# Expert rows turned by VectorE in 32x32 blocks, and first-layer expert weights read as one 8 KB run per partition

## The chip, the cores and the metric

The kernel runs on one core of a Trainium2 chip. The metric is the device time of one execution in microseconds (us), lower is better. Three runs of the kernel before took 1007.83, 1006.43 and 1007.63 us; the median is 1007.63 us.

## The reference, cut to what matters

Two decoder layers over x of shape (8, 100, 512), all float32: self-attention, cross-attention to a context of 722 rows, and a feed-forward part, each followed by a residual and a layer norm. The change lies in the feed-forward part of the first layer, a mixture of 8 experts. Each of the 800 rows picks its two best experts by a softmax gate. An expert is three 512x512 layers:

    h1 = relu(row @ w1[e] + b1[e])
    h2 = relu(h1 @ w2[e] + b2[e])
    y  = relu(gate * (h2 @ w3[e] + b3[e]))

The kernel needs the sum of y over the rows of a tile of one expert, and hands that sum back to every row that chose the expert.

## The kernel before, in words

The whole program is one sequence of blocks. A block gives each engine its own instruction list; the engines meet at a barrier at its end. This case concerns two neighbouring blocks.

**The routing block** (from line 1784). The gate is computed, the 800 rows (512 features and 8 gate values, so XW = 520 floats or 2080 bytes) are scattered into DRAM by expert (`rows_dram`), and a table gives for each of MT = 20 tiles of 128 rows its expert and its first row. Under this, TensorE folds weights of a later layer (`fold_one`, lines 1899 to 1941). SyncE (the SP queue) loads the weights of the first three units, waits for the scatter and for the fold step "bvo", and then issues `gather(0)` to `gather(5)` (AHEAD = 6, lines 1995 to 2003). `gather` (line 1780) reads the tile's row number from the table and copies 128 whole rows into SBUF, one row to a partition, by one DMA.

**The expert block** (from line 2044). Each tile i goes through three layers l. The 60 pairs (i, l) are the units. They are ordered on a slant (line 1676): after the start, units repeat as (i,0), (i-1,1), (i-2,2), which is called a round here. For i of 1 and more, unit (i,0) is number 3(i-1). The weights of a unit are 1 MB, w[e] of 512x512, in a ring of six slots; SP loads unit n when unit n-6 is made (`load_unit`, lines 1684 and 2055). `expert_w` (line 1675) splits the 512 input features as chunk c, partition p, feature 128c+p, so a partition gets four runs of 2 KB. After the load, from n = 5 on, SP issues one more gather per unit until all 20 are out, then one of six loads for the next stage per unit (`last`, lines 2047 to 2063).

For a matrix product over features, the features must lie on the partitions, but a gathered tile has rows there. So TensorE turns tile i by four 128x128 transposes into PSUM (`turn`, line 2069), ScalarE copies them to `xh` (`keep`, line 2143), and the first layer waits for the semaphore `kept`. The order on TensorE is written out by hand: ahead of the unit before (i,0), it does `turn(i)` (lines 2118 to 2121). A unit is `layer(n)` (line 2102): 4 output chunks times 4 feature chunks, 16 matmuls of 128x128 by 128. ScalarE applies bias and relu after layer 0 (line 2155), VectorE after layer 1 (`second_layer`, line 2198), and VectorE adds bias and multiplies by the gate after layer 2 (`weigh`, line 2213). GpSimd picks the gate values of a tile (line 2247), VectorE sums them (`gate_of`), and TensorE spreads them by one small matmul at each l = 1 unit (`spread_gate`, line 2084). From unit 39 on (PREP_AT), ScalarE and VectorE also prepare weights of the next stage: `in_kv` is waited for by VectorE at n = 39 and `in_qup` by ScalarE at n = 40.

Of the kernel before, what the change touches and what calls it, by code (L numbers as in the profile page):

```python
# [23 lines left out]
P = 128  # L24
# [90 lines left out]
def program(nc, g, out):  # L115
    ctx = ExitStack()
    with ctx:
# [1557 lines left out]
        expert_w = [g[f"L0_ffn_w{i}"].rearrange("e (c p) o -> p e c o", p=P) for i in (1, 2, 3)]  # L1675
# [89 lines left out]
        AHEAD = 6  # L1765
# [12 lines left out]
        gathered = [sem(f"rows_gathered{i}") for i in range(MT)]  # L1778

        def gather(sp, i):  # L1780
            row = sp.value_load(table[0:1, 1, i:i + 1], min_val=0, max_val=SPARE)
            sp.dma_start(rows_of_tile(i), rows_dram[bass.ds(row, P), :]).then_inc(gathered[i], 16)

        with nc.Block() as block:
# [210 lines left out]
            @block.sync  # L1995
            def _(sp):
                sp.wait_ge(chain, CH["table"])
                for n in range(NL):
                    load_unit(sp, n, expert_of(sp, units[n][0]))
                sp.wait_ge(scattered, 16 * 2 * B)  # L2000
                sp.wait_ge(folded, fold_at["bvo", 0] + 1)
                for i in range(AHEAD):
                    gather(sp, i)
# [13 lines left out]
        xh, h1, h2 = (sb("ffn_" + n, [P, 2, C, P], F32, ff) for n in ("xh", "h1", "h2"))  # L2017
# [5 lines left out]
        turned, kept, made, h1_kept, h2_kept, gated, gate_col, gate_rows, rows_kept, weighed, counted, v_flip, v_hi, v_lo, by_tile, tile_kept = (  # L2023
            sem("ffn_" + s) for s in ("turned", "kept", "made", "h1_kept", "h2_kept", "gated", "gate_col", "gate_rows",
# [10 lines left out]
        def unit_made(eng, i, l):  # L2035

            eng.wait_ge(made, unit_at[i, l] + 1)
# [6 lines left out]
        with nc.Block() as block:  # L2044
            @block.sync
            def _(sp):
                last = [(rk, natural(g["L1_attn_Wk"]), in_kv), (rv, natural(g["L1_attn_Wv"]), in_kv),
                        (rd, g["L1_attn_W_down_kv"].rearrange("(c p) l -> p c l", p=P), in_qup),
                        (ru, g["L1_attn_W_up_k"].rearrange("l (c d) -> l c d", c=C), in_qup),
                        (rw, g["L1_attn_W_up_v"].rearrange("l (c d) -> l c d", c=C), in_qup),  # L2050
                        (rq, natural(g["L1_attn_Wq"]), in_qup)]
                more = AHEAD
                for n in range(NL, len(units)):
                    expert = expert_of(sp, units[n][0])
                    if n >= SLOTS:
                        sp.wait_ge(made, n - SLOTS + 1)
                    load_unit(sp, n, expert)
                    if n >= SLOTS - 1 and more < MT:
                        gather(sp, more)
                        more += 1  # L2060
                    elif more == MT and last:
                        to, src, landed = last.pop(0)
                        sp.dma_start(to if to is rw else to[:], src).then_inc(landed, 16)
                for s in range(SLOTS):
                    sp.wait_ge(w_landed[s], 16 * (len(units) // SLOTS))

            @block.tensor
            def _(pe):
                def turn(i):
                    pe.wait_ge(gathered[i], 16)  # L2070
                    if i >= 2:
                        pe.wait_ge(kept, i - 1)
                    for c in range(C):
                        mm = nc.tensor.transpose(ps[:, 3 + i % 2, c * P:(c + 1) * P], rows_of_tile(i)[:, c * P:(c + 1) * P],  # L2074
                                                 ident[:, :])
                    mm.then_inc(turned, 1)

# [24 lines left out]
                def layer(n):  # L2102
# [6 lines left out]
                    for m in range(C):  # L2109
                        for k in range(C):  # L2110
                            if l and m == 0:
                                pe.wait_ge((h1_kept, h2_kept)[l - 1], C * i + k + 1)
                            mm = nc.tensor.matmul(acc(n)[:, m, :], w[:, n % SLOTS, k, m * P:(m + 1) * P],  # L2113
                                                  into[l][:, i % 2, k, :], start=k == 0, stop=k == C - 1,
# [3 lines left out]
                turn(0)  # L2118
                for n, (i, l) in enumerate(units):
                    if n + 1 < len(units) and units[n + 1][1] == 0:  # L2120
                        turn(units[n + 1][0])
# [20 lines left out]
            def _(act):  # L2142
                def keep(i):
                    act.wait_ge(turned, i + 1)
                    if i >= 2:
                        unit_made(act, i - 2, 0)
                    nc.scalar.activation(xh[:, i % 2, :, :], ps[:, 3 + i % 2, :].rearrange("p (c t) -> p c t", c=C),  # L2147
                                         ACT.Identity).then_inc(kept, 1)

# [14 lines left out]
                keep(0)  # L2164
                for n, (i, l) in enumerate(units):
                    if n + 1 < len(units) and units[n + 1][1] == 0:
                        keep(units[n + 1][0])
# [29 lines left out]
            def _(dve):  # L2197
                def second_layer(n, i):
# [22 lines left out]

                for n, (i, l) in enumerate(units):
                    if l == 0:
# [18 lines left out]
            def _(pool):  # L2242
                for i in range(MT):
                    pool.wait_ge(gathered[i], 16)
# [871 lines left out]
```

## Time and profile before, and how to read it

| what | value |
| --- | --- |
| median of three runs | 1007.63 us |
| span of the profiled execution, first to last instruction | 1003.7 us |
| TensorE busy over the span (matmuls, weight loads) | 934.0 us (93%), 757.2 us (75%) |
| VectorE, ScalarE, GpSimd busy | 429.3, 346.5, 250.9 us |
| mean granted TensorE clock over the span | 0.957 of full |
| data moved by DMA | 162.01 MB, mean 161 GB/s |

The profiled execution has no time of its own beside its span of 1003.7 us; the median of the runs lies 3.9 us above that span, which is time around the first and last instruction. PE is TensorE's matmul side, PEld its weight loads, DVE VectorE, ACT ScalarE, POOL GpSimd, SPq the queue of SyncE. A float32 matmul shows as two PE and two PEld records (passes), so a unit has 32 of each. Matmuls are pipelined and their ends are modelled: the distance between starts says what one costs, not its duration.

### The profile page before, as it was taken

How to read it: one execution, taken by the hardware profiler on the slowest of the kernel's cores; microseconds unless marked ns; L12 is line 12 of the kernel's file. 1: busy time of each engine (PE TensorE's matmuls, PEld its weight loads, DVE VectorE, ACT ScalarE, POOL GpSimd, SP SyncE). 2: the span in 40 equal slices, each digit the busy share in tenths (PEclk: the TensorE clock that was granted, in tenths of full speed). 3: DMA queues.
4: the chain of work that ended last, by engine and by line, in shares of the span. 5: the costliest groups of instructions: out<-in, count | busy, mean ns of one | idle time of the engine just before them, and what ended most of it. 6: DMA issues, size and time to landing. Idle time of an engine off the chain costs nothing. (4 is left out here: it accounts for less than half of the span.)

```text
span 1003.7 us, 19227 instructions
## 1 busy us (share of the span) xinstructions
PE 934.0 (93%) x7747; PEld 757.2 (75%) x7747; DVE 429.3 (43%) x994; ACT 346.5 (35%) x886; POOL 250.9 (25%) x306
## 2 busy tenths in 40 slices
PE   5999999989998889999999999999889899999994
PEld 5977776676775644789999999987765578999532
DVE  2973454224442647002112132135267630656576
ACT  2322323245552124122222233324276611122374
POOL 5452111023554306000000010004065403000275
PEclk9999999999999979899999999997969998999996
DMA  9994000245622807259999888700040032971001
GB/s 254 382 331 127 2 2 2 98 152 203 238 120 95 309 7 254 55 181 386 358 383 313 284 269 283 254 29 28 4 153 3 2 119 78 321 247 66 1 15 51
DMA packets 72456, 162.01 MB, mean 161 GB/s; under 512 B 4132, under 2 KB 5685, under 8 KB 70321
## 3 DMA queue, kind: packets, MB, share of 16 engines
q1 hardware_dynamic: 70048, 156.54, 45.8%
q0 software_dynamic: 2320, 4.25, 1.4%
q8 instruction: 61, 1.00, 0.4%
q14 instruction: 27, 0.21, 0.1%
HBM read 128.81 MB, written 31.97 MB: 160 GB/s over the span
## 5 line engine op out<-in xcount | busy, mean ns | idle before, releaser
L2113 PE MATMUL ps<-ffn_h,ffn_w 128*128 128x128 f32 x1280 | 149.1, 275 | 0.0
L2113 PEld LDWEIGHTS ps<-ffn_h,ffn_w 128*128 128x128 f32 x1280 | 145.9, 192 | 0.0
L2113 PE MATMUL ps<-ffn_xh,ffn_w 128*128 128x128 f32 x640 | 74.9, 275 | 0.3 <-ACT ffn_xh L2147 0.3
L2203 DVE TENSOR_SCALAR ffn_h<-ps,tile_bias 128x128 f32<-128x128 f32 x80 | 22.5, 345 | 122.4 <-PE ps L2113 122.4
L2113 PEld LDWEIGHTS ps<-ffn_xh,ffn_w 128*128 128x128 f32 x640 | 73.1, 192 | 0.9 <-issue 0.9
L1418 POOL TENSOR_TENSOR ctx_low<-shelf,ctx_high 128x1024 fp32r<-128x1024 f32 (+2 forms) x24 | 43.0, 1819 | 65.4 <-PE ps L1283 33.7
L2161 ACT ACTIVATE ffn_y<-ffn_y 128x128 f32<-128x128 f32 x80 | 23.7, 298 | 73.9 <-DVE ffn_y L2219 73.9
L1526 PE MATMUL ps<-x_qT,ctx_ct 128*128 128x100 f32 (+1 forms) x384 | 46.4, 284 | 2.3 <-PEq L137 2.0
L1526 PEld LDWEIGHTS ps<-x_qT,ctx_ct 128*128 128x128 f32 (+1 forms) x384 | 45.0, 197 | 3.7 <-issue 3.2
L2219 DVE SCALAR_TENSOR_TENSOR ffn_y<-ps,tile_bias,ffn_gate_row 128x128 f32<-128x128 f32 x80 | 22.6, 344 | 58.0 <-PE ps L2113 57.9
L2834 POOL TENSOR_TENSOR att_e<-att_e,decay 100x400 f32<-100x400 f32 x32 | 32.7, 1033 | 46.1 <-DVE att_e L2685 46.1
L111 PE MATMUL ps<-ctx_ct,x_qT 128*100 128x210 f32 (+1 forms) x128 | 40.3, 467 | 1.0 <-DVE ctx_ct L1432 0.7
L2155 ACT ACTIVATE ffn_h<-ps,tile_bias 128x128 f32<-128x128 f32 x80 | 22.8, 368 | 41.6 <-PE ps L2113 41.6
L3007 POOL TENSOR_TENSOR rstd<-rstd,minus_half 100x1 f32<-100x1 f32 x16 | 11.6, 740 | 99.6 <-DVE rstd L2950 95.0
L111 PEld LDWEIGHTS ps<-ctx_ct,x_qT 128*100 128x100 f32 x128 | 20.6, 166 | 18.7 <-issue 17.4
L2781 ACT ACTIVATE att_e<-att_e,att_mx 100x100 f32<-100x100 f32 x96 | 28.1, 365 | 15.5 <-DVE att_mx L2690 15.5
L1538 PE MATMUL ps<-ctx_pT,shelf 128*128 128x100 f32 (+1 forms) x288 | 33.2, 275 | 0.2 <-ACT xf L1571 0.2
L1538 PEld LDWEIGHTS ps<-ctx_pT,shelf 128*128 128x128 f32 (+1 forms) x288 | 32.6, 192 | 0.4 <-issue 0.4
L1565 ACT ACTIVATE ctx_pk<-ctx_pk,ctx_st 128x100 f32<-128x100 f32 x48 | 13.8, 365 | 54.9 <-DVE ctx_st L1601 54.9
L2906 PE MATMUL ps<-x_n,xf 128*100 128x512 f32 x64 | 29.9, 596 | 0.6 <-PEq L1507 0.6
L111 PE MATMUL ps<-l_ro,xf 128*100 128x512 f32 x64 | 29.7, 608 | 0.0
L2147 ACT ACTIVATE ffn_xh<-ps 128x512 f32<-128x512 f32 x20 | 11.8, 598 | 49.1 <-PE ps L2074 49.1
(469 smaller groups left out, 2096.8 us busy)
## 6 DMA issues: line engine op xcount, KB each, us to landing
ffn_w<-in_L_ffn_w_dram SPq DMA_DIRECT2D x60, 1024.0 KB, 6.0
shelf<-in_ctx_dram SPq DMA_DIRECT2D x12, 1280.0 KB
expert_rows<-nothing SPq DMA_DIRECT2D x1, 14820.0 KB, 49.6
context_turned<-ctx_ct SPq DMA_DIRECT2D x8, 1444.0 KB, 7.9
ctx_ct<-context_turned SPq DMA_DIRECT2D x8, 1444.0 KB, 12.5
ctx_lent<-in_ctx_dram SPq DMA_DIRECT2D x4, 1280.0 KB
rows_own<-expert_rows SPq DMA_DIRECT2D x8, 260.0 KB, 3.0
x_wo<-in_L_xattn_Wo_dram SPq DMA_DIRECT2D x1, 2048.0 KB, 9.5
```

The costliest lines, as they stand in the source:

```text
L111: last = pe.matmul(out, a, b, start=(n == 0), stop=(n == len(products) - 1))
L1418: nc.gpsimd.tensor_tensor(raw_low[b % RAWS][0:rows_, j0:j1, :], raw[b % RAWS][0:rows_, j0:j1, :], raw_high[b % 2][0:rows_, j0:j1, :].bitca ...
L1526: mm = nc.tensor.matmul(ps[0:rows_, SB + i, (j - j0) * T:(j - j0 + 1) * T], ct[b % 2][:, k, j * P:j * P + rows_], qT[:, k, b * T:(b + 1) * T],
L1538: mm = nc.tensor.matmul(ps[:, VB, c * T:(c + 1) * T], raw[b % RAWS][0:keys(j), j, c * P:(c + 1) * P], pT[0:keys(j), b % 2, j, :], start=j ...
L2113: mm = nc.tensor.matmul(acc(n)[:, m, :], w[:, n % SLOTS, k, m * P:(m + 1) * P], into[l][:, i % 2, k, :], start=k == 0, stop=k == C - 1, sk ...
L2155: nc.scalar.activation(h1[:, i % 2, m, :], acc(n)[:, m, :], ACT.Relu, bias=bsel[:, m, i, 0:1]).then_inc(h1_kept, 1)
L2161: nc.scalar.activation(y[:, i % 2, m, :], y[:, i % 2, m, :], ACT.Relu, accum_out=vT[:, m, i:i + 1]).then_inc(counted, 1)
L2203: nc.vector.tensor_scalar(h2[:, i % 2, m, :], acc(n)[:, m, :], bsel[:, m, i, 1:2], 0.0, ALU.add, ALU.max).then_inc(h2_kept, 1)
L2219: nc.vector.scalar_tensor_tensor(y[:, i % 2, m, :], acc(n)[:, m, :], bsel[:, m, i, 2:3], gate_row[:, i % 2, :], ALU.add, ALU.mult).then_in ...
L2781: ins = nc.scalar.activation(e[:, c, :], e[:, c, :], ACT.Exp, bias=mx[:, b % 2, r, c:c + 1])
L2834: nc.gpsimd.tensor_tensor(e, e, decay[:, :].unsqueeze(1).to_broadcast([T, C, T]), ALU.mult).then_inc(faded, 1)
L2906: mm = nc.tensor.matmul(ps[0:T, b % 3, :], xf[:, k, b * T:(b + 1) * T], n1[:, k, :], start=k == 0, stop=False)
```

## The change: what it does

- The DMA of a tile's features is cut into four, one per group f of 32 partitions. Each writes 32 partitions with four pieces of 512 bytes: partition 32f+r gets, for i = 0 to 3, features 128f to 128f+127 of row 32i+r. A fifth DMA brings the 8 gate values of each row (32 bytes a partition), with a semaphore of its own that GpSimd waits for.
- VectorE then turns the 16 blocks of 32x32 in one instruction. It reads the features with a step of four (16 bytes), so that after it partition p holds, for chunk k, feature 4p+k of all 128 rows. `xh` is laid out as [partition, row group, chunk, 32].
- The first layer's weights are split the same way, feature 4p+k, so that partition p gets rows 4p to 4p+3 of w1 as one run of 8 KB. Its matmuls read `xh` as four runs of 32 floats. The other two layers are unchanged.
- TensorE's `turn` and ScalarE's `keep` are gone, and the PSUM banks 3 and 4 with them.
- Three tiles are gathered in the routing block in place of six. The rest follow one per round, at the l = 1 units from n = 4 on; the six `last` loads follow at the l = 2 units 26, 29, ... 41.

```diff
-        expert_w = [g[f"L0_ffn_w{i}"].rearrange("e (c p) o -> p e c o", p=P) for i in (1, 2, 3)]
+        first_w = g["L0_ffn_w1"].rearrange("e (p c) o -> p e c o", c=C)
+        group = lambda f: slice(f * HD, (f + 1) * HD)
+        expert_w = [first_w] + [g[f"L0_ffn_w{i}"].rearrange("e (c p) o -> p e c o", p=P) for i in (2, 3)]
...
-        AHEAD = 6
+        AHEAD, EARLY = 6, 3
...
         def gather(sp, i):
             row = sp.value_load(table[0:1, 1, i:i + 1], min_val=0, max_val=SPARE)
-            sp.dma_start(rows_of_tile(i), rows_dram[bass.ds(row, P), :]).then_inc(gathered[i], 16)
+            here = rows_dram[bass.ds(row, P), :]
+            for f in range(HPC):
+                sp.dma_start(rows_of_tile(i)[group(f), 0:D].rearrange("r (i d) -> r i d", d=P),
+                             here[:, f * P:(f + 1) * P].rearrange("(i r) d -> r i d", r=HD)).then_inc(gathered[i], 16)
+            sp.dma_start(rows_of_tile(i)[:, D:XW], here[:, D:XW]).then_inc(gathered_gates[i], 16)
...
-                for i in range(AHEAD):
+                for i in range(EARLY):
                     gather(sp, i)
...
-        xh, h1, h2 = (sb("ffn_" + n, [P, 2, C, P], F32, ff) for n in ("xh", "h1", "h2"))
+        xh = sb("ffn_xh", [P, 2, HPC, C, HD], F32, ff)
+        h1, h2 = (sb("ffn_" + n, [P, 2, C, P], F32, ff) for n in ("h1", "h2"))
...
-                    if n >= SLOTS - 1 and more < MT:
+                    if more < MT and units[n][1] == 1:
                         gather(sp, more)
                         more += 1
-                    elif more == MT and last:
+                    elif n >= 4 * SLOTS and units[n][1] == 2 and last:
                         to, src, landed = last.pop(0)
...
-                def turn(i):
-                    pe.wait_ge(gathered[i], 16)
-                    if i >= 2:
-                        pe.wait_ge(kept, i - 1)
-                    for c in range(C):
-                        mm = nc.tensor.transpose(ps[:, 3 + i % 2, c * P:(c + 1) * P], rows_of_tile(i)[:, c * P:(c + 1) * P],
-                                                 ident[:, :])
-                    mm.then_inc(turned, 1)
...
+                            rhs = xh[:, i % 2, :, k, :] if l == 0 else into[l][:, i % 2, k, :]
                             mm = nc.tensor.matmul(acc(n)[:, m, :], w[:, n % SLOTS, k, m * P:(m + 1) * P],
-                                                  into[l][:, i % 2, k, :], start=k == 0, stop=k == C - 1,
+                                                  rhs, start=k == 0, stop=k == C - 1,
...
-                def keep(i):
-                    act.wait_ge(turned, i + 1)
-                    if i >= 2:
-                        unit_made(act, i - 2, 0)
-                    nc.scalar.activation(xh[:, i % 2, :, :], ps[:, 3 + i % 2, :].rearrange("p (c t) -> p c t", c=C),
-                                         ACT.Identity).then_inc(kept, 1)
...
+                def turn(i):
+                    dve.wait_ge(gathered[i], 16 * HPC)
+                    if i >= 2:
+                        unit_made(dve, i - 2, 0)
+                    nc.vector.transpose(xh[:, i % 2], rows_of_tile(i)[:, 0:D].rearrange("p (i d k) -> p i k d", i=HPC, k=C)
+                                        ).then_inc(kept, 1)
...
+                turn(0)
                 for n, (i, l) in enumerate(units):
+                    if n + 1 < len(units) and units[n + 1][1] == 0:
+                        turn(units[n + 1][0])
                     if l == 0:
                         gate_of(i)
...
-                    pool.wait_ge(gathered[i], 16)
+                    pool.wait_ge(gathered_gates[i], 16)
```

## Rows read from the trace of the kernel before

**Rows 1.** Busy time by stage: stretch, length, then each engine, clock, DMA share, GB/s.

```profile
core 0: us, PE busy (x) PEld busy (x) DVE busy (x) ACT busy (x) POOL busy (x), PEclk, DMA share, GB/s
439.00:672.00 233.00, 232.62 (x2080) 231.94 (x2081) 52.03 (x183) 68.71 (x290) 5.45 (x16) 1.00 0.85 291
```

**Rows 2.** Timeline of one round: start, duration, engine, line, operation, count, idle before.

```profile
481.56 0.60 PE L2074 MATMUL ps<-ident,rows_own 128*128 128x128 f32 x4
481.76 1.13 DVE L2203 TENSOR_SCALAR ffn_h<-ps,tile_bias 128x128 f32<-128x128 f32 x4 [6.11 <-PE ps L2113]
...
482.00 3.74 PE L2113 MATMUL ps<-ffn_h,ffn_w 128*128 128x128 f32 x32
...
485.57 3.74 PE L2113 MATMUL ps<-ffn_xh,ffn_w 128*128 128x128 f32 x32
...
489.14 0.39 PE L2084 MATMUL ps<-ident,ffn_gate 128*128 128x128 f32 x2
...
489.37 3.74 PE L2113 MATMUL ps<-ffn_h,ffn_w 128*128 128x128 f32 x32
```

**Rows 3.** Timeline of PE where the expert block begins.

```profile
436.57 0.40 PE L111 MATMUL ps<-x_wk_hi,x_wq_lo 128*128 128x512 f32 x1
437.90 1.07 PE L2074 MATMUL ps<-ident,rows_own 128*128 128x128 f32 x8 [0.94 <-PEq L1784]
439.31 0.91 PE L2113 MATMUL ps<-ffn_xh,ffn_w 128*128 128x128 f32 x6 [0.34 <-ACT ffn_xh L2147]
```

**Rows 4.** Instructions on the copied tile: duration min/median/max in ns, first and last start.

```profile
L2147 ACT ACTIVATE ffn_xh<-ps x20: 592/597/614, 438.6 to 642.8; 128x512 f32<-128x512 f32 x20
```

**Rows 5.** Timeline of DVE in the expert block, other work of its kind.

```profile
589.40 2.28 DVE L2231 TENSOR_TENSOR l_raw_k<-l_raw_k,l_raw_v 128x2048 f32<-128x2048 f32 x1
...
600.71 0.68 DVE L2236 TENSOR_TENSOR l_pu_lo<-l_raw_up_k,l_pu_hi 128x512 fp32r<-128x512 f32 x1
...
607.98 1.22 DVE L2236 TENSOR_TENSOR l_pq_lo<-l_raw_q,l_pq_hi 128x1024 fp32r<-128x1024 f32 x1
```

**Rows 6.** Timeline of PEld in the routing block, weight loads between float32 passes of 512 columns.

```profile
400.43 0.19 PEld L111 LDWEIGHTS ps<-x_woT,x_wv 128*128 128x128 f32 x1 [0.24 <-issue]
...
400.86 0.19 PEld L111 LDWEIGHTS ps<-x_woT,x_wv 128*128 128x128 f32 x1 [0.24 <-issue]
```

**Rows 7.** DMA issues of SP in time order: table reads between them, and none.

```profile
419.48 5.86 SPq L1782 DMA_DIRECT2D rows_own<-expert_rows  x6
438.57 2.69 SPq L1687 DMA_DIRECT2D ffn_w<-in_L_ffn_w_dram  x3
...
674.06 0.42 SPq L2256 DMA_DIRECT2D spreads<-in_spreads_dram  x1
674.53 0.43 SPq L2257 DMA_DIRECT2D l_ro<-in_L_attn_Wo_dram  x1
```

**Rows 8.** Issue to landing, page: weights, row tiles, the last load (KB each, median us).

```profile
ffn_w<-in_L_ffn_w_dram SPq DMA_DIRECT2D x60, 1024.0 KB, 6.0
...
xT_hi<-expert_rows SPq DMA_DIRECT2D x6, 260.0 KB, 8.3
...
l_raw_q<-in_L_attn_Wq_dram SPq DMA_DIRECT2D x1, 1024.0 KB, 12.3
```

**Rows 9.** DMA from 450 to 470 us: 2 KB runs, engines full.

```profile
q1 hardware_dynamic: 3947, 7.72, 104.6%
```

**Rows 10.** DMA from 674.5 to 675.1 us: 128 runs of 512 bytes and 16 smaller.

```profile
q1 hardware_dynamic: 144, 0.07, 37.6%
```

**Rows 11.** DMA from 815 to 832 us: runs of 11.5 KB.

```profile
q1 hardware_dynamic: 288, 2.96, 47.9%
```

**Rows 12.** Busy time and clock after a pause of PE, columns as in rows 1.

```profile
677.00:678.00 1.00, 0.00 (x0) 0.00 (x0) 0.93 (x3) 0.58 (x1) 0.28 (x2) 1.00 1.02 375
678.00:680.00 2.00, 1.71 (x6) 1.02 (x6) 1.61 (x4) 0.73 (x2) 1.26 (x4) 0.50 0.64 240
...
684.00:690.00 6.00, 5.13 (x17) 3.51 (x17) 4.82 (x10) 3.51 (x6) 2.51 (x9) 0.50 0.00 0
```

More of the change, by code:

```diff
@@ L1777, in program @@
         fold_bank = lambda n: ps[:, (7, 0, 1)[n % 3], :]
-        gathered = [sem(f"rows_gathered{i}") for i in range(MT)]
+        gathered, gathered_gates = ([sem(f"{what}_gathered{i}") for i in range(MT)] for what in ("rows", "gates"))
         def gather(sp, i):
             row = sp.value_load(table[0:1, 1, i:i + 1], min_val=0, max_val=SPARE)
-            sp.dma_start(rows_of_tile(i), rows_dram[bass.ds(row, P), :]).then_inc(gathered[i], 16)
+            here = rows_dram[bass.ds(row, P), :]
[3 more added lines that the diff above has]
+            sp.dma_start(rows_of_tile(i)[:, D:XW], here[:, D:XW]).then_inc(gathered_gates[i], 16)
         with nc.Block() as block:
@@ L2022, in program @@
         vT = sb("ffn_vT", [P, C, MT], F32, ff)
-        turned, kept, made, h1_kept, h2_kept, gated, gate_col, gate_rows, rows_kept, weighed, counted, v_flip, v_hi, v_lo, by_tile, tile_kept = (
-            sem("ffn_" + s) for s in ("turned", "kept", "made", "h1_kept", "h2_kept", "gated", "gate_col", "gate_rows",
+        kept, made, h1_kept, h2_kept, gated, gate_col, gate_rows, rows_kept, weighed, counted, v_flip, v_hi, v_lo, by_tile, tile_kept = (
+            sem("ffn_" + s) for s in ("kept", "made", "h1_kept", "h2_kept", "gated", "gate_col", "gate_rows",
                                       "rows_kept", "weighed", "counted", "v_flip", "v_hi", "v_lo", "by_tile", "tile_kept"))
@@ L2051, in _ @@
                         (rq, natural(g["L1_attn_Wq"]), in_qup)]
-                more = AHEAD
+                more = EARLY
                 for n in range(NL, len(units)):
@@ L2057, in _ @@
                     load_unit(sp, n, expert)
-                    if n >= SLOTS - 1 and more < MT:
+                    if more < MT and units[n][1] == 1:
                         gather(sp, more)
                         more += 1
-                    elif more == MT and last:
+                    elif n >= 4 * SLOTS and units[n][1] == 2 and last:
                         to, src, landed = last.pop(0)
                         sp.dma_start(to if to is rw else to[:], src).then_inc(landed, 16)
+                assert more == MT and not last
                 for s in range(SLOTS):
@@ L2112, in layer @@
                                 pe.wait_ge((h1_kept, h2_kept)[l - 1], C * i + k + 1)
+                            rhs = xh[:, i % 2, :, k, :] if l == 0 else into[l][:, i % 2, k, :]
                             mm = nc.tensor.matmul(acc(n)[:, m, :], w[:, n % SLOTS, k, m * P:(m + 1) * P],
-                                                  into[l][:, i % 2, k, :], start=k == 0, stop=k == C - 1,
+                                                  rhs, start=k == 0, stop=k == C - 1,
                                                   skip_group_check=True)
                     mm.then_inc(made, 1)
-                turn(0)
                 for n, (i, l) in enumerate(units):
-                    if n + 1 < len(units) and units[n + 1][1] == 0:
-                        turn(units[n + 1][0])
                     if l == 1:
@@ L2162, in total @@
                                              accum_out=vT[:, m, i:i + 1]).then_inc(counted, 1)
-                keep(0)
                 for n, (i, l) in enumerate(units):
-                    if n + 1 < len(units) and units[n + 1][1] == 0:
-                        keep(units[n + 1][0])
                     if 0 <= n - PREP_AT - 1 < len(PREP):
```

## The prediction

> **What bounds the kernel now.** I read the busy time by stage first. From 439 to 672 us the expert block runs, and there TensorE's matmuls are busy 232.62 of 233 us at full granted clock (1.00) while VectorE is busy 52 us and ScalarE 69 us; the 16 DMA engines show a share of 0.85 [rows 1]. So this block lasts as long as TensorE's own list of instructions, and something taken off that list shortens it if nothing else comes to the front. Then I read the timeline of one round for what each entry of that list costs [rows 2]. The reader should look at starts: a unit takes 485.57 - 482.00 = 3.57 us, and so does the next (489.14 - 485.57). The four transposes of a turn hold the list from 481.56 to 482.00, 0.44 us. The gate's small matmul holds it from 489.14 to 489.37, 0.23 us. A round is 3 x 3.57 + 0.44 + 0.23 = 11.38 us. Third, the beginning of the block: the last pass of the routing block starts at 436.57 and ends at 436.97, TensorE goes on at 437.90 with two turns, and the first unit starts at 439.31, after ScalarE's copy [rows 3]. That copy starts at 438.6 and takes 0.60 us [rows 4], so from its end to the first pass there is about 0.1 us.
>
> **Part 1, the turns leave TensorE.** Of 20 turns, 18 lie between units; each gives back 0.44 us: 18 x 0.44 = 7.9 us. This is on the path that sets the end, since TensorE has no idle time there to absorb it. A round becomes 10.94 us.
>
> **Part 2, the start.** Turns 0 and 1 lie ahead of the first unit. In the changed kernel the first unit waits for VectorE's first turn, which can begin when the barrier opens, as TensorE does now at 437.90. The trace has no turn on VectorE. Its nearest rows: one instruction over 512 elements a partition from SBUF takes 0.68 us, over 1024 elements 1.22, over 2048 elements 2.28 [rows 5]. I take 0.69 us, by the row with the same 512 elements. The bounds: from half of that, were two elements moved at a time, to 2.28, were each element of the stepped read to cost as much as four. With 0.69 and the hop of 0.1, the first unit starts at 438.69 in place of 439.31: 0.6 us gained, with bounds from 0.95 gained to 0.97 lost.
>
> **Part 3, where the later turns lie on VectorE.** Turn i stands behind the four instructions of `second_layer` and ahead of `weigh`. In rows 2 `second_layer` starts 0.20 us after the unit before it is done (481.76 against 481.56) and lasts 1.13. The next first layer is due 3.57 us after the same point. That leaves 3.57 - 1.33 - 0.10 = 2.14 us for a turn, so 0.69 us is hidden by the unit of layer 2 that TensorE runs meanwhile; without that cover each turn would cost its full length. One place is tighter: the preparation of later weights puts 1.22 us between, starting at 607.98 [rows 5], which is 0.20 + 1.04 = 1.24 us after a unit is done (the four instructions of `second_layer` take 1.13 us with the end of the last). The turn is done at 607.98 + 1.22 + 0.69 + 0.10 = 609.99, while the unit is due near 607.98 - 1.24 + 3.57 = 610.31. It still fits. VectorE waits now for the gather; behind that wait stand `weigh` and `gate_of`, and for these ScalarE's sums and the gate matmul, so a late tile would hold the whole chain. ScalarE loses 20 copies of 0.60 us, which nobody on the path waited for: nothing.
>
> **Part 4, the gathers on SP.** With a table read between, DMA issues stand (5.86 - 0.35) / 5 = 1.1 us apart, loads (2.69 - 0.38) / 2 = 1.16; without one, 674.53 - 674.06 = 0.47 [rows 7]. A gather of five DMAs is 1.1 + 4 x 0.47 = 3.0 us, at most 5.5 if each costs 1.1. In the routing block, three take 9 us (at most 16.5) from 419.48, so they are out before TensorE's last pass ends at 436.97 [rows 3, 7]: nothing, the fold matmuls are the cover. In the expert block a round asks SP for 3 loads and one gather, 3.5 + 3.0 = 6.5 us (at most 9.0) of 10.94: the queue keeps up, and a load behind a gather goes out up to 0.6 us late. Tile i is issued when unit 3i-11 is made and turned after unit 3i-5: six units, 21 us, against 3 to 5.5 us of issue and 8.3 us of landing [rows 8]. Hidden.
>
> **Part 5, what the DMA engines carry.** A weight load has five units, 17.9 us, from issue to use and lands in 6.0 [rows 8], so 11.9 us are to spare. That is why the 8 KB run itself is worth nothing here. Per packet: full engines spent 1.046 x 16 x 20 us / 3947 = 85 ns on a 2 KB run [rows 9]; a 512-byte run alone cost 0.376 x 16 x 0.6 / 144 = 25 ns [rows 10]; a run of 10.3 KB on average 0.479 x 16 x 17 / 288 = 452 ns [rows 11], so 8 KB some 360. A round then asks (1024 x 85 + 128 x 360 + 640 x 25) / 16 = 9.3 us of each engine, in 10.94: nothing. The six loads for the next stage add at most 512 x 85 / 16 = 2.7 us to a round, which the 11.9 us absorb. The last of them goes out when unit 35 is made and is needed after unit 39: 14.3 us against the 12.3 that it took to land among other traffic [rows 8]. It fits.
>
> **Part 6, the passes over four runs of 32.** No row shows a matmul that reads its moving operand in runs. Four passes of 128 columns take 4 x 3.57 / 32 = 0.446 us, one of 512 columns 400.86 - 400.43 = 0.43 [rows 2, 6], so a break between instructions costs 5 ns at most. If a break between runs cost as much, three in each of 640 first-layer passes are 640 x 3 x 5 = 10 us; a gain is excluded, since no column falls away. I take nothing: a new instruction brings new weights, a new run only a new address.
>
> **The sum**, against the profiled execution: 7.9 + 0.6 = 8.5 us from its span of 1003.7 gives 995.2. The runs' median lies 3.9 us above that span, and I keep this: **999.1 us**.
>
> **The rivals.** *The clock falls at the start.* TensorE now pauses from 436.97 to 438.69, 1.7 us, in place of 0.9 and 0.3. After 677 us a pause of about that length is followed by a clock of 0.50 up to 690 [rows 12], that is 1.2 in place of 2.4 GHz. Were it so here for up to 12 us, up to 6 us would be lost; I price it at 4, the forecast becoming 1003. Against it: the same place had 0.9 and 0.3 us of pause before, and the block ran at 1.00 all the same [rows 1, 3]. *The turn is slow.* VectorE reads with a step of 16 bytes. At 2.28 us the start loses 0.97, each of the 18 later turns is 0.14 late, 2.5 in all, and the tight place 1.3: 7.9 - 0.97 - 2.5 - 1.3 = 3.1 us gained, about 1004.5. At 1.22 us only about 0.7 of the 8.5 us would go. No row shows a stepped read of this kind. The Trainium skill, Advanced Engine Details and Errata, section SBUF Cachelines, says that SBUF answers in lines of 16 bytes and that a read whose every access falls in a new line pays for it, which speaks against this change. It states no price; rows 5 show dense reads only. *The small packets starve the weights*, the case on the slower side. Its place is the DMA engines between 447 and 640 us. If a packet of a gather costs p ns among other traffic, a round asks 8.3 + 0.040 p us, and 17 rounds with a gather run 17 x (8.3 + 0.040 p - 10.94) us into arrears, of which 11.9 are covered. It eats the gain of 8.5 from p = 96 ns on, and at 110 ns the kernel takes 1017 us. For it: VectorE, SP and TensorE would all wait behind one late tile. Against it: 25 ns alone [rows 10], and even the 85 ns of a 2 KB run on full engines [rows 9] leave the gain nearly whole. *The runs cost a break each* (part 6): at the whole 10 us the result is 1009.
>
> **How the numbers follow.** The forecast has 0.71, the clock 0.10, the slow turn 0.08, the small packets 0.06, the runs 0.05. A measurement of this kernel can tell about 0.2%, 2 us, from no change. The first three cases are all faster by more: 0.89, of which I move 0.01 to the others for what I have not seen; the runs' case splits between same and slower. So faster 0.88, same 0.03, slower 0.09. The range reaches from 996.5, the forecast with the better start and the spread of 1.4 us of the runs, to 1004.5, which holds the clock and the slow turn and leaves the last two out.
>
> **What would show it.** No transposes on TensorE between 439 and 664 us, and passes of a unit still 3.57 us apart, in first layers too. A round of 10.94. One instruction of VectorE per tile, near 0.69 us, ended before the unit that needs it is due. The first unit near 438.7, at clock 1.00. Weight loads landing well within 17.9 us. I am wrong if TensorE shows idle time ahead of first layers (named after VectorE or a gather), if it waits for weights, or if first-layer passes are wider apart than the others.

## The result, and the profile after

The changed kernel takes **999.76 us** in the median of 11 runs (995.55 to 1004.6); the kernel before, run beside it, 1006.86 us. The ratio is 0.9942, 95% interval [0.9922, 0.9963]; it is formed from the runs, while the quotient of the two medians is 0.9930. The forecast was 999.1 us. In two later sets of runs on one chip each, the same kernel stood at 0.9929 [0.9909, 0.9948] and 0.9912 [0.9887, 0.9937] to the kernel before. (Of the 11 runs of before, one took 2871.49 us and was disturbed; without it their median is 1006.65 us.)

The profiled execution took 995.55 us with a span of 993.8. First, TensorE's list of one round, and VectorE's turn beside it, from the timeline of the changed kernel (start, duration, engine, line, operation, count, idle time before):

```profile
493.42 1.09 DVE L2191 STREAM_TRANSPOSE ffn_xh<-rows_own 128x512 f32<-128x512 f32 x1
...
495.75 3.74 PE L2114 MATMUL ps<-ffn_xh,ffn_w 128*128 128x128 f32 x32
...
499.32 0.39 PE L2084 MATMUL ps<-ident,ffn_gate 128*128 128x128 f32 x2
...
503.32 1.13 DVE L2199 TENSOR_SCALAR ffn_h<-ps,tile_bias 128x128 f32<-128x128 f32 x4 [6.08 <-PE ps L2114]
504.36 1.09 DVE L2191 STREAM_TRANSPOSE ffn_xh<-rows_own 128x512 f32<-128x512 f32 x1
```

The transposes of [rows 2] are gone from PE. A first-layer unit still holds the list for 499.32 - 495.75 = 3.57 us, so its four runs of 32 columns cost nothing. With the gate's 0.22 and two more units the next first layer is due 10.94 us later, at 506.69; the turn for it ends at 504.36 + 1.09 = 505.45. It is hidden, with 1.2 us to spare.

Second, the same timeline where the expert block begins, where it ends, and at VectorE's first turns:

```profile
436.11 0.40 PE L111 MATMUL ps<-x_wk_hi,x_wq_lo 128*128 128x512 f32 x1
438.67 5.44 PE L2114 MATMUL ps<-ffn_xh,ffn_w 128*128 128x128 f32 x32 [2.16 <-DVE ffn_xh L2191]
444.04 0.54 PE L2129 MATMUL ps<-indT,tile_expert_turned 8*20 8x400 f32 x2
...
664.68 0.61 PE L2135 MATMUL ps<-ident,ffn_vT 128*20 128x128 f32 x4
```

```profile
437.45 2.05 DVE L2191 STREAM_TRANSPOSE ffn_xh<-rows_own 128x512 f32<-128x512 f32 x2 [42.92 <-PEq L1791]
```

This answers to [rows 3]. TensorE stands still for 2.16 us in place of 0.94 and 0.34, and then the first unit holds the list for 444.04 - 438.67 = 5.37 us; in a kernel without that pause it takes 3.74 (below). The busy time by stage says why (stretch, length, busy time of PE, PEld, DVE, ACT, POOL, granted clock, DMA share, GB/s):

```profile
438.00:439.00 1.00, 0.33 (x2) 0.36 (x2) 1.00 (x2) 0.00 (x0) 0.00 (x0) 0.85 0.00 0
439.00:442.00 3.00, 3.00 (x16) 3.00 (x16) 0.61 (x3) 0.00 (x0) 0.20 (x1) 0.50 0.97 322
442.00:444.00 2.00, 2.00 (x18) 1.91 (x17) 0.00 (x0) 0.00 (x0) 0.00 (x0) 0.97 0.75 274
444.00:600.00 156.00, 156.00 (x1395) 155.61 (x1395) 49.10 (x139) 41.04 (x189) 3.19 (x14) 1.00 1.04 336
```

The granted clock is 0.50 (1.2 of 2.4 GHz) from about the start of the first unit and back at 1.00 shortly after 442 us, before that unit ends. From there TensorE is busy without a gap up to 600 us. The DMA share is 1.04, where before it was 0.97 from 446 to 600 us. The page's row on the weight loads, from issue to landing (KB each, median us), stands against 6.0 in [rows 8]:

```profile
ffn_w<-in_L_ffn_w_dram SPq DMA_DIRECT2D x60, 1024.0 KB, 9.6
```

The slowest took 14.1 us, of the 17.9 that a load has.

**Where the 9.9 us between the two profiled spans went.** I use three landmarks: the end of the routing block's last pass, the first unit, and the last transposes of the block, on `ffn_vT`. The row for these in the timeline of PE of the kernel before:

```profile
671.43 0.60 PE L2137 MATMUL ps<-ident,ffn_vT 128*20 128x128 f32 x4
```

| stretch | before | after | gained |
| --- | --- | --- | --- |
| span's start to the last pass's end | 436.97 | 436.51 | 0.46 |
| that pass to the first unit | 2.34 | 2.16 | 0.18 |
| first unit to the last transposes | 232.12 | 226.01 | 6.11 |
| last transposes to the span's end | 332.27 | 329.12 | 3.15 |

Only the second and third rows, 6.29 us, belong to the change. The first is where the routing block happened to end (435.0 to 440.8 us in the 13 profiles of this study). The 0.46 us were there before the change can act: the gate's matmuls, at the head of the block, start at 352.83 us before and at 352.30 after, and from there to the last pass's end it is 84.14 and 84.21 us. Part of that spread is the clock too. In the changed kernel's first profile it fell to 0.50 while a pause of 2.38 us near 363 us still ran; in its second it fell only some 2.6 us after the end of the same pause, and there the same way took 87.01 us. The last row is, in these two profiles, a fall of the clock at another barrier, 170 us behind the change, which some executions have and some don't, whatever the kernel. Timeline of PE there, before and then after, and busy time over ten microseconds of it, columns as above, again before and then after:

```profile
841.83 8.62 PE L1526 MATMUL ps<-x_qT,ctx_ct 128*128 128x100 f32 x48 [1.97 <-PEq L137]
```

```profile
834.82 5.37 PE L1526 MATMUL ps<-x_qT,ctx_ct 128*128 128x100 f32 x48 [1.97 <-PEq L137]
```

```profile
840.00:850.00 10.00, 8.17 (x45) 8.20 (x46) 0.39 (x3) 0.49 (x1) 8.19 (x7) 0.66 0.41 147
```

```profile
830.00:840.00 10.00, 8.03 (x64) 7.73 (x62) 0.65 (x3) 1.19 (x2) 5.20 (x5) 1.00 0.39 128
```

The same 48 matmuls after the same pause of 1.97 us took 8.62 us or 5.37: 3.25 us. In the 13 profiles they took 8.6 us six times, 7.0 twice and 5.4 five times, at a mean clock of 0.60, 0.76 and 1.00. In all 13 profiles the last stretch is 332.2 to 332.3 us (five times, two of them the changed kernel's repeats), 331.1 to 331.4 (three) or 328.6 to 329.1 (five); one of the middle three had the 8.6 us and was quicker elsewhere. So a comparison of two profiled spans is worth 3 us more or less by this alone, and below, the stretch from the first unit to the last transposes, called the **stage** here, is what is compared. It holds what the first unit loses.

6.29 us of 1006.86 would be a ratio of 0.9938. The first two intervals hold it, the third ends at 0.9937.

### The profile page after: what moved, and what is told of

Its sections match the earlier page's. It is cut to its first block and busy times, and to the rows that moved or that the text cites. A ratio compares the mean times of both kernels' runs of the same rounds, so it can differ in the third digit from the quotient of the medians.

```text
span 993.8 us, 19289 instructions
## 1 busy us (share of the span) xinstructions
PE 923.1 (93%) x7667; PEld 746.0 (75%) x7667; DVE 450.0 (45%) x1014; ACT 335.4 (34%) x866; POOL 249.5 (25%) x306
## 5 line engine op out<-in xcount | busy, mean ns | idle before, releaser
L2114 PE MATMUL ps<-ffn_h,ffn_w 128*128 128x128 f32 x1280 | 146.4, 275 | 0.0
L1526 PE MATMUL ps<-x_qT,ctx_ct 128*128 128x100 f32 (+1 forms) x384 | 43.1, 272 | 2.3 <-PEq L137 2.0
L1526 PEld LDWEIGHTS ps<-x_qT,ctx_ct 128*128 128x128 f32 (+1 forms) x384 | 41.7, 185 | 3.7 <-issue 3.2
L2191 DVE STREAM_TRANSPOSE ffn_xh<-rows_own 128x512 f32<-128x512 f32 x8 | 8.6, 1087 | 47.5 <-PEq L1791 42.9
```

What stands on the lines that cost most here:

```text
L1526: mm = nc.tensor.matmul(ps[0:rows_, SB + i, (j - j0) * T:(j - j0 + 1) * T], ct[b % 2][:, k, j * P:j * P + rows_], qT[:, k, b * T:(b + 1) * T],
```

## The experiments

The theory after this reading: the turns are gone as forecast and hidden on VectorE; what is missing is the pause at the start, through the clock (theory A). The rival was that the DMA engines, now full, delay loads or tiles (theory B). The change again (its first run), the first early turn, the busy TensorE and the whole rows ran on one chip, beside the kernel before at 1005.33 us; the dense and the doubled turn, the four runs and the 8 KB run alone beside it at 1005.41; the other three kernels on another chip, beside it at 1006.37.

**The change again.** The changed kernel unedited, twice, to stand beside the others.

> The changed kernel once more, unaltered, for a second profile. Theory A (the pause): after the barrier TensorE stands idle for about 2.2 us until VectorE has turned tile 0, its clock then drops to half, and the first unit takes about 5.4 us in place of 3.57; the rest of the block runs at 10.94 us a round, and the stage from the first unit to the last transposes of the block is about 226 us again. Theory B (the small packets): the DMA engines are full, and in some executions weights or tiles come late; then this profile shows TensorE waiting for weights or for VectorE inside the block, in another place than the start. The time against before lies between 0.992 and 0.996 by either.

> The changed kernel once more, to stand beside the run above: pause 2.16 us, first unit 5.4 us long, 226.0 us from first unit to last transposes, about 999 us, ratio to before near 0.9935.

Measured: 998.74 us, ratio 0.9929 [0.9909, 0.9948], pause 2.16 us, stage 666.05 - 440.03 = 226.02; then 999.4 us, 0.9912 [0.9887, 0.9937], pause 2.17, stage 669.00 - 442.99 = 226.01. The stage repeats to 0.01 us, the total does not (the runs spread over 993.98 to 1003.01). A loss that is the same to 0.01 us each time is not one of chance traffic on the DMA engines.

**The first two turns earlier.** VectorE turns tiles 0 and 1 at the end of its list in the routing block, when they have landed, and the expert block begins with the matmuls. (`xh` and the semaphore `kept` are made earlier for this, which the cut leaves out.)

```diff
+                for i in range(2):
+                    dve.wait_ge(gathered[i], 16 * HPC)
+                    nc.vector.transpose(xh[:, i], rows_of_tile(i)[:, 0:D].rearrange("p (i d k) -> p i k d", i=HPC, k=C)
+                                        ).then_inc(kept, 1)
...
-                turn(0)
                 for n, (i, l) in enumerate(units):
-                    if n + 1 < len(units) and units[n + 1][1] == 0:
+                    if 1 < n + 1 < len(units) and units[n + 1][1] == 0 and units[n + 1][0] >= 2:
```

> Tiles 0 and 1 are turned at the end of the routing block's VectorE list, under the fold matmuls, so the first unit waits for the barrier alone. Theory A: TensorE's pause falls from 2.2 to about 1 us, the first unit starts some 1.1 us earlier after the barrier's opening, the clock stays at 1.00 and the first unit takes 3.57 us: 1.1 + 1.8 = 2.9 us less than the changed kernel. Theory B: only the 1.1 us of the start, or nothing, since the time that is missing is lost at the DMA engines.

> The kernel with the first two turns made in the routing block, a second time. Theory A (the pause of 2.16 us costs 1.63 us of clock, and the turn itself another 1.07 of the gap): first unit about 1.1 us after the last pass of the routing block, at clock 1.00, 224.4 us from the first unit to the last transposes; 2.7 us less than the changed kernel beside it, ratio to before near 0.991, but the 5 us by which runs of one kernel differ can hide part of this. Rival (what was gained the first time was chance): the two medians within 1 us.

Measured: 995.25 us, ratio 0.9917 [0.9887, 0.9947]; the second time 994.89, 0.9887 [0.9871, 0.9903], beside 999.4 for the changed kernel. Timeline of PE, and busy time over the first unit, of the first of them:

```profile
439.08 3.81 PE L2118 MATMUL ps<-ffn_xh,ffn_w 128*128 128x128 f32 x32 [1.09 <-PEq L1792]
442.82 0.53 PE L2133 MATMUL ps<-indT,tile_expert_turned 8*20 8x400 f32 x2
...
663.46 0.61 PE L2139 MATMUL ps<-ident,ffn_vT 128*20 128x128 f32 x4
```

```profile
439.08:442.82 3.74, 3.74 (x32) 3.62 (x32) 0.32 (x2) 0.00 (x0) 0.41 (x3) 1.00 0.55 166
```

The pause is the barrier's 1.09 us alone, the clock stays at 1.00, the first unit takes 3.74 us, and the stage is 663.46 - 439.08 = 224.38 us: 1.63 less than 226.01, as theory A says, with as many gathers and as full engines (a share of 1.05 from 446 to 600 us, against 1.04). With the pause, 1.63 + 1.07 = 2.7 us. The medians differ by 3.5 and 4.5 us; the part above 2.7 lies within what runs of one kernel differ by. This version is the fastest of the study.

The second profile of it shows theory B too, once. Its stage is 225.14 us; timeline of PE:

```profile
593.27 3.84 PE L2118 MATMUL ps<-ffn_xh,ffn_w 128*128 128x128 f32 x32 [0.29 <-DMA ffn_w<-in_L_ffn_w_dram]
...
597.17 7.64 PE L2118 MATMUL ps<-ffn_h,ffn_w 128*128 128x128 f32 x64
604.64 3.74 PE L2118 MATMUL ps<-ffn_xh,ffn_w 128*128 128x128 f32 x32
```

A weight load came 0.3 us late, and two units behind it took 604.64 - 597.17 = 7.47 us in place of 7.14, with PEld waiting for a load as well. The longest landing there was 15.4 us. Part of it is SP's queue: the load for the unit at 593.27 could go out when the unit that starts at 570.92 is made, at 574.5, but SP was at a gather from 571.18 to 576.17 and at two more loads, and issued it at 580.00, 5.5 us late. So the loads are in time with little in hand near 590 us, where the loads for the next stage ride along; it cost some 0.76 us in this one execution, and nothing in the other profiles of kernels with this kind of gather and one turn a tile.

**TensorE kept busy through the wait.** The turns stay where the change put them; ten small matmuls (128x128 by 128) whose result nobody uses stand ahead of the units on TensorE.

```diff
+                keep_array_busy(10)
                 for n, (i, l) in enumerate(units):
                     if l == 1:
                         spread_gate(i)
```

> TensorE multiplies ten 128x128 blocks that nobody reads before it waits for the first turn; everything else is the changed kernel. Theory A: the first unit starts when it did (about 1.2 us after VectorE's turn begins), but the clock stays at 1.00 and the unit takes 3.57 us: 1.8 us less than the changed kernel. If the pause has nothing to do with the clock, the first unit still takes about 5.4 us and the time is the changed kernel's.

Measured: 997.26 us, ratio 0.9925 [0.9901, 0.9949], against 998.74 for the changed kernel on the same chip. Timeline of PE:

```profile
434.58 0.40 PE L111 MATMUL ps<-x_wk_hi,x_wq_lo 128*128 128x512 f32 x1
435.91 1.30 PE L553 MATMUL ps<-identR 128*128 128x128 f32 x10 [0.94 <-PEq L1791]
437.15 3.81 PE L2114 MATMUL ps<-ffn_xh,ffn_w 128*128 128x128 f32 x32
...
661.54 0.61 PE L2136 MATMUL ps<-ident,ffn_vT 128*20 128x128 f32 x4
```

The first unit comes 437.15 - 434.98 = 2.17 us after the last pass, as late as in the changed kernel, and yet the clock stays at 1.00 and the stage is 661.54 - 437.15 = 224.39. So the 1.63 us are the clock's alone, not those of tiles or weights that arrive late. This is what the kernel before had without meaning to: its turns stood in the same place [rows 3]. The matmuls leave TensorE idle for only 2.17 - 1.24 = 0.93 us there, so the runs do not tell whether the longest pause or the sum of the pauses counts.

**A pause between.** The early turn, with a VectorE copy that TensorE waits for before its first unit.

```diff
+                pe.wait_ge(paused, 1)
                 for n, (i, l) in enumerate(units):
...
+                nc.vector.tensor_copy(spare[:, :, :, :], xh[:, 0, 0:2]).then_inc(paused, 1)
```

> The early turn, with TensorE made to wait once more at the start for a VectorE copy of 256 elements a partition (an added instruction, whose result nobody uses) so that the pause is about 1.5 us, between the 1.09 after which the clock stayed at 1.00 and the 1.80 after which it fell. Theory A (what decides is how long TensorE stands still): either the first unit takes 3.7 us and the stage 224.4, or 5.4 and 226.0; the run says which side 1.5 us lies on. Rival (the fall comes from waiting for the turn or from what VectorE does, not from the length of the pause): the stage stays at 224.4 whatever the pause.

Measured, in one execution: the pause came out at 1.33 us, not 1.5, the clock stayed at 1.00 and the stage is 666.07 - 441.66 = 224.41. So waiting for VectorE does not by itself cost the clock; but as 1.33 us cost nothing, this run alone does not part theory A from the rival. The busy TensorE does: VectorE did the same turns there, and the clock stayed. In this place 1.33 us cost nothing and 1.80 (next experiment) cost the full 1.63. Between them it is open, and it holds for this place alone: at the later barrier 1.97 us went both ways, and behind the expert block eleven of the 13 profiles have a pause of 1.6 us and a clock of 0.50 after it ([rows 12] is one), while in the other two the clock was down already ahead of it.

**The same turn, read densely.** Each block reads 32 features side by side. One execution.

```diff
-                    nc.vector.transpose(xh[:, i % 2], rows_of_tile(i)[:, 0:D].rearrange("p (i d k) -> p i k d", i=HPC, k=C)
+                    nc.vector.transpose(xh[:, i % 2], rows_of_tile(i)[:, 0:D].rearrange("p (i k d) -> p i k d", i=HPC, k=C)
```

> VectorE's turn reads each block of 32 features side by side in place of one feature in four; so the chunks meet the wrong weight rows, and nothing else changes. Theory A (the read with a step of 16 bytes is what makes the turn 1.09 us): the instruction takes about 0.69 us like a copy of 512 elements, TensorE's pause at the start shrinks from 2.16 to about 1.76 us. Rival B (the block transpose costs 1.09 us whatever it reads): 1.09 us, pause 2.16, first unit 5.4 us long at a clock that falls to 0.50. Under A a first unit of 3.7 to 3.8 us would say that a pause of 1.76 does not yet cost the clock. Either way the rest of the stage stays as it was, 10.94 us a round.

Measured, instructions on the turned tile (duration min/median/max in ns, first and last start), first this kernel and then the changed one:

```profile
L2191 DVE STREAM_TRANSPOSE ffn_xh<-xT_hi x6: 699/703/704, 514.8 to 569.5; 128x512 f32<-128x512 f32 x6
```

```profile
L2191 DVE STREAM_TRANSPOSE ffn_xh<-xT_hi x6: 1092/1097/1101, 515.3 to 570.0; 128x512 f32<-128x512 f32 x6
```

The step of 16 bytes costs 1.097 - 0.703 = 0.39 us, a factor of 1.56; the block transpose itself costs about what a pass over the same 512 elements does (0.68 in [rows 5]). Timeline of PE in this kernel:

```profile
438.15 5.44 PE L2114 MATMUL ps<-ffn_xh,ffn_w 128*128 128x128 f32 x32 [1.80 <-DVE ffn_xh L2191]
443.52 0.53 PE L2129 MATMUL ps<-indT,tile_expert_turned 8*20 8x400 f32 x2
...
664.02 0.61 PE L2135 MATMUL ps<-ident,ffn_vT 128*20 128x128 f32 x4
```

The pause shrank to 1.80 us, and the first unit still took 443.52 - 438.15 = 5.37: the slow read is not what cost the clock. The total was 998.14 us. The stage is 664.02 - 438.15 = 225.87, 0.14 less than 226.01, and that is the tight place. In the changed kernel the round there is longer than 10.94 us:

```profile
597.81 0.39 PE L2084 MATMUL ps<-ident,ffn_gate 128*128 128x128 f32 x2
...
605.24 3.81 PE L2114 MATMUL ps<-ffn_xh,ffn_w 128*128 128x128 f32 x32
608.88 0.39 PE L2084 MATMUL ps<-ident,ffn_gate 128*128 128x128 f32 x2
```

That is 608.88 - 597.81 = 11.07 us; with the dense read the same round takes 10.95.

**Every turn twice.** One execution.

```diff
+                    for sem_ in (once, kept):
                         nc.vector.transpose(xh[:, i % 2], rows_of_tile(i)[:, 0:D].rearrange("p (i d k) -> p i k d", i=HPC, k=C)
-                                        ).then_inc(kept, 1)
+                                            ).then_inc(sem_, 1)
+                        if sem_ is once:
+                            dve.wait_ge(once, i + 1)
```

> Every turn is done twice on VectorE, one after the other, 2.2 to 2.3 us in place of 1.09. Theory A (the later turns are hidden under the layer 2 unit, with some 1.2 us to spare in an ordinary round and 0.1 in the tight place near 604): ordinary rounds go from 10.94 to at most 11.05 us, the tight place loses about 1.2 us, the start about 1.1 us plus what the clock takes: 2.5 to 5 us more for the whole, the length from the first unit to the last transposes growing from 226.0 to 227 to 229. Rival C (VectorE's turn is on the path): each of the 18 later turns costs its 1.1 us again, some 20 us more.

Measured: 1002.65 us, stage 669.64 - 439.27 = 230.37, 4.36 more than 226.01: a little above what A allowed, far from C's 20. Timeline of PE in this kernel:

```profile
439.27 6.51 PE L2115 MATMUL ps<-ffn_xh,ffn_w 128*128 128x128 f32 x32 [3.27 <-DVE ffn_xh L2193]
...
468.31 0.39 PE L2085 MATMUL ps<-ident,ffn_gate 128*128 128x128 f32 x2
...
479.39 0.39 PE L2085 MATMUL ps<-ident,ffn_gate 128*128 128x128 f32 x2
```

and what PE waited for from 436 to 672 us (us in total, times, longest):

```profile
PE ps L2115 <- DVE ffn_xh L2193: 4.3, 2, 3.3
```

Rounds are 479.39 - 468.31 = 11.08 us, 0.14 longer than 10.94: with two turns in 2.24 us each first layer comes late (by too little for a row of idle time of its own), which puts the cover at about 2.1 us. Over 17 rounds that is 2.4 us; the tight place near 607 us is the second wait, 4.3 - 3.3 = 1.0 us; and after the longer pause of 3.27 us the first unit took 6.51 - 5.44 = 1.1 us more. Together 4.5, against 4.36 measured. So one turn of 1.09 us is covered in an ordinary round, a second one is not.

**What the DMA engines carry**, three kernels. Whole rows in one DMA a tile, as before, into the changed kernel (VectorE and GpSimd wait for that one):

```diff
-            for f in range(HPC):
-                sp.dma_start(rows_of_tile(i)[group(f), 0:D].rearrange("r (i d) -> r i d", d=P),
-                             here[:, f * P:(f + 1) * P].rearrange("(i r) d -> r i d", r=HD)).then_inc(gathered[i], 16)
-            sp.dma_start(rows_of_tile(i)[:, D:XW], here[:, D:XW]).then_inc(gathered_gates[i], 16)
+            sp.dma_start(rows_of_tile(i), here).then_inc(gathered[i], 16)
```

> Each tile comes by one DMA of whole rows again, as before the change (so the turned tiles hold the wrong features), all else as in the changed kernel. Theory A: the DMA share of the block falls from about 1.04 to about 0.95 and weights land sooner than 9.6 us, but the time stays within 1 us of the changed kernel, since TensorE waits for neither. Theory B: 2 us or more less than the changed kernel.

Then the changed kernel with the first layer's weights in four runs of 2 KB, and the kernel before with the 8 KB run alone:

```diff
-        first_w = g["L0_ffn_w1"].rearrange("e (p c) o -> p e c o", c=C)
+        first_w = g["L0_ffn_w1"].rearrange("e (c p) o -> p e c o", p=P)
```

> The first layer's weights come again as four runs of 2 KB a partition, with the features split the other way than the turned rows (that alone is changed). Theory A (the 8 KB run is worth nothing for the time): 998 to 1000 us, stage from first unit to last transposes 226.0, loads landing in about 10 us with the DMA engines full, none late. Rival D (with the small packets of the gathers the engines have no room left, and the 8 KB run is what kept the loads in time): loads land in 14 us or more, TensorE waits for weights between 450 and 640, stage 228 or longer, 1001 us or more.

```diff
-        expert_w = [g[f"L0_ffn_w{i}"].rearrange("e (c p) o -> p e c o", p=P) for i in (1, 2, 3)]
+        first_w = g["L0_ffn_w1"].rearrange("e (p c) o -> p e c o", c=C)
+        expert_w = [first_w] + [g[f"L0_ffn_w{i}"].rearrange("e (c p) o -> p e c o", p=P) for i in (2, 3)]
...
-                        mm = nc.tensor.transpose(ps[:, 3 + i % 2, c * P:(c + 1) * P], rows_of_tile(i)[:, c * P:(c + 1) * P],
+                        mm = nc.tensor.transpose(ps[:, 3 + i % 2, c * P:(c + 1) * P], rows_of_tile(i)[:, 0:D].rearrange("p (d k) -> p k d", k=C)[:, c, :],
```

> The kernel before, with the 8 KB run alone: first-layer weights split as feature 4p+k and TensorE's four transposes reading every fourth column; gathers, ScalarE's copies and the order stay as before. Theory A: the same time as before within 0.2%, round 11.38 us, loads landing in about 6 us. Rival D (the longer run is a gain of its own): 2 us or more faster. A third possibility: the transposes read with a step and cost TensorE more, a round above 11.38 by up to 0.4 us, up to 8 us slower.

Measured: whole rows 1000.2 us, ratio 0.9939 [0.9919, 0.996], stage 666.70 - 440.69 = 226.01. Four runs 997.09 us, 0.9929 [0.9906, 0.9951], stage 663.11 - 437.12 = 225.99. Before with the 8 KB run 1005.52 us beside 1005.41, **0.9999 [0.9985, 1.0013]**. In the changed kernel neither packet size moves the stage by more than 0.02 us, and this stage is what decides. By their totals alone the first misses theory A's 1 us (it is 1.5 us above the first repeat's 998.74) and the second its 998 to 1000, both by less than runs of one kernel differ. The DMA view from 450 to 470 us (queue: packets, MB, share of 16 engines) of the changed kernel, of whole rows, and of four runs:

```profile
DMA packets 3811, 6.80 MB, mean 340 GB/s; under 512 B 512, under 2 KB 1536, under 8 KB 3552
...
q1 hardware_dynamic: 3808, 6.76, 106.1%
```

```profile
q1 hardware_dynamic: 2826, 7.11, 97.5%
```

```profile
q1 hardware_dynamic: 4502, 6.61, 102.2%
```

Without the small packets of the gathers the share here is 97.5%, with more bytes moved (from 446 to 600 us it is 0.97 against 1.04), and the median weight load lands in 6.9 us; with them it takes 9.6, and with four runs of 2 KB 10.1, which is within the 9.1 to 11.3 us of the other profiles with these gathers, 8 KB runs and one turn a tile. (The doubled turn, whose rounds are 0.14 us longer, had 7.4.) In the kernel before, the 8 KB run did not shorten the landing: 7.1 us, against 6.0 in [rows 8]. Even the slowest of all these, 15.4 us, lies under the 17.9 us that a load has if it is issued on time. In the kernel before, the transposes that read every fourth column held TensorE 0.48 us in place of 0.44 [rows 2] (480.49 - 480.01):

```profile
480.01 0.64 PE L2075 MATMUL ps<-ident,rows_own 128*128 128x128 f32 x4
480.49 3.74 PE L2114 MATMUL ps<-ffn_h,ffn_w 128*128 128x128 f32 x32
```

Over 18 turns that is 0.7 us, and its stage is 670.52 - 437.64 = 232.88, 0.76 longer than before. That is the third possibility named ahead of the run, in small; a gain from the 8 KB run of that size would be hidden by it here, but not in the kernel with four runs, whose stage is the changed kernel's.

## Why the prediction was right, and where it was not

- **Part 1, the turns leave TensorE: right.** With the clock kept (early turn, filler) the stage is 224.38 us against 232.12, 7.74 us for 18 turns, 0.43 each; 7.9 was forecast.
- **Part 2, the start: the step that failed.** The turn was taken at 0.69 us "by the row with the same 512 elements" and took 1.09: that row is right for a dense read, which measured 0.70, and wrong for a step of 16 bytes. TensorE's pause was 2.16 us in place of the 1.72 worked out, so the gain at the start is 2.34 - 2.16 = 0.18 us, not 0.6, and the clock took 1.63 us of the next unit, which the sum had at nothing. That the first unit began at 438.67, where 438.69 was forecast, is chance: the routing block ended 0.46 us earlier in that execution.
- **The rival on the clock came true**, and stands in the forecast at a chance of 0.10. It was priced at 4 us from a stretch of up to 12 us at 0.50; the clock came back within the first unit, and the price was 1.63. The evidence held against it, that before had "0.9 and 0.3 us of pause" and a clock of 1.00, does not bear on the new pause: 0.94 + 0.34 = 1.28 us in two pieces is less than 1.72 by either count. Here, with ten matmuls in the pause, or with a pause of 1.09 us, the clock stayed; with 1.80 us or more in one piece it fell each time.
- **Part 3, later turns hidden: right.** The slack of 2.14 us is what the doubled turn measured (2.24 us late by 0.14 a round). The tight place fits with the 0.69 us assumed, as the dense turn's 0.70 shows, but not quite with 1.09: the turn that starts at 603.99 ends at 605.10, the unit starts at 605.24, and the round is 0.13 us longer.
- **The rival of the slow turn: right in its cause, small in its price.** The dense turn shows that the step costs 0.39 us. The Trainium skill, Advanced Engine Details and Errata, section SBUF Cachelines, says that an access to a new 16-byte line each time is penalized; the trace agrees, at 1.10 us against 0.70. Past the start and the tight place it lands on VectorE's free time; those two lost 0.44 and 0.14 us, near the 0.7 that the rival gave for a turn of 1.22.
- **Part 4, SP: right in its outcome, too low in its figures.** In the changed kernel a gather's five issues take 2.4 to 3.4 us up to 532 us (2.5 from 482.72 to 485.24; 3.0 forecast), but 3.3 to 5.6 from 537 us on (forecast at most 5.5). No tile was late. That a load goes out at most 0.6 us late did not hold: in the second early turn one went out 5.5 us late, and it came late.
- **Part 5, the DMA engines: a term was mis-sized.** The small packet was taken at 25 ns from a stretch where it ran alone [rows 10]. From 450 to 470 us the engines spent 1.061 x 16 x 20 = 339.5 us; 2016 runs of 2 KB at 85 ns and 259 longer ones at 360 ns take 264.6 of that, which leaves 74.9 / 1536 = 49 ns for each small packet. That is an estimate from one stretch, and the 360 ns in it is one too; but the kernel with four runs, which has no runs of 8 KB, gives the same: its 2966 runs of 2 KB leave (327.0 - 252.1) / 1536 us, or 49 ns. It goes with landings of 9.6 in place of 6.0 us. By it a round asks (8.3 + 0.040 x 49) = 10.3 us of 10.94: still enough, with little in hand. The 8 KB run is worth nothing for the time, as forecast (0.9999).
- **Part 6, runs of 32: right.** A first-layer unit holds TensorE's list for 3.57 us, as the others do.

The sum: forecast 8.5; measured 7.74 + 0.18 - 1.63 = 6.29. So the gain was 2.2 us smaller than forecast, and that the median still came out 0.7 us from the forecast is luck. The 3.9 us that the forecast kept between span and median is not time around the first and last instruction: every run of the changed kernel took 1.74 to 1.84 us longer than its own span, and the runs of before that have both figures 1.75 to 2.97. The rest says that the profiled execution of before was quicker than the median run, and the runs of either kernel spread over some 6 to 9 us.

## What to carry to other kernels

Work taken off the engine that sets the time also takes away what filled its pauses. Where a change makes TensorE wait for another engine at the head of a stage, compare its new idle time there with what the kernel had, price a fall of the clock from rows at both levels, and do the first piece ahead of the barrier: here two early turns were worth 2.7 us on top of the change's 6.3. And compare profiled stages by landmarks before and behind them, since here the time ahead of the stage differed by up to 6 us from profile to profile and the time behind it by over 3.

## What the runs showed of the hardware that was not expected

- One pause of 1.80 to 2.17 us ahead of the expert block took the granted clock to 0.50 in all six profiles that had it, and one of 3.27 us did in the seventh; pauses up to 1.33 us in that place never did, and neither did 2.17 us with ten small matmuls within it. At a later barrier, 1.97 us did so in some executions and not in others.
- VectorE's 32x32 block transpose of 128x512 float32 took 0.70 us with a dense read and 1.10 us with a step of 16 bytes.
- TensorE's transposes, too, were slower when they read every fourth column: 0.48 us for four in place of 0.44.
